# Group norm and attention, one core: query products that go on in a copied PSUM bank, with a new order on VectorE

## What is computed

```python
xn = group_norm(x, gamma, beta)              # 32 groups, eps 0.001
xf = xn.reshape(B, N, C)                     # N = 1024 tokens, C = 512
q = xf @ wq + bq
k = xf @ wk + bk
v = xf @ wv + bv
scores = jnp.einsum('bnc,bmc->bnm', q, k) * C ** (-0.5)
attn = jax.nn.softmax(scores, axis=-1)
out = jnp.einsum('bnm,bmc->bnc', attn, v)
out = out @ wp + bp
return out.reshape(B, H, W, C) + residual    # residual = x
```

## Time and profile before

| | us |
|---|---|
| median of 3 runs (lowest, highest) | 2137.26 (2137.19, 2137.89) |
| the profiled execution's own time | 2139.97 |
| its span in the profile | 2138.3 |

### The profile page before, as it was taken

One profiled execution on the slowest core, in us unless ns is written; L12 is line 12 of the kernel. 1 busy time (PEld: TensorE's weight loads), 2 busy tenths in 40 slices (PEclk: granted clock), 3 DMA queues, 4 the chain that ended last, 5 costly groups with the idle time before them and its releaser, 6 DMA issues.

```text
span 2138.3 us, 28427 instructions
## 1 busy us (share of the span) xinstructions
PE 2099.0 (98%) x9253; PEld 1730.9 (81%) x9253; DVE 1798.7 (84%) x2554; ACT 743.7 (35%) x1216; POOL 877.3 (41%) x475
## 2 busy tenths in 40 slices
PE   7999999999999999999999999999999999999999
PEld 5877888888888888888888788888878888888887
DVE  6898897988979888888888979889788898888865
ACT  4242332423333243332523324233332433335232
POOL 2452442524335244443524425243352434435253
PEclk9999999999999999999999999999999999999999
DMA  8003012030300203012030120303012030120101
GB/s 211 20 11 109 1 54 64 15 103 0 94 24 34 83 0 118 0 49 69 10 108 0 56 62 15 103 0 93 25 34 83 0 118 0 49 69 10 69 1 60
DMA packets 110268, 108.13 MB, mean 51 GB/s; under 512 B 8476, under 2 KB 74016, under 8 KB 110240
## 3 DMA queue, kind: packets, MB, share of 16 engines
q1 hardware_dynamic: 107984, 103.58, 16.0%
q10 hardware_dynamic: 2256, 4.20, 0.8%
HBM read 74.19 MB, written 33.55 MB: 50 GB/s over the span
## 4 chain that ended last, share of the span: by engine, by line
PE 51%; DVE 19%; issue 18%; POOL 7%; ACT 3%; DMA 0%; POOLq 0%; DVEq 0%; ACTq 0%
PE psum L1226 6%; PE psum L1228 6%; PE psum L1227 6%; PE psum L1251 5%; PE psum L1253 5%; PE psum L1252 5%; PE psum L1140 4%; PE psum L1139 4%; PE psum L1137 4%; DVE pt_lo L694 4%; POOL total_part L449 4%; DVE score L869 3%; DVE xn_lo L694 3%; POOL total_part L458 2%; PE psum L1057 2%
## 5 line engine op out<-in xcount | busy, mean ns | idle before, releaser
L1251 PE MATMUL psum<-v_hi,pt_hi 128*128 128x512 f32 x1024 | 401.4, 392 | 20.6 <-DVE pt_lo L694 17.4
L426 POOL TENSOR_TENSOR x_res<-x_res,out_bias 128x512 f32<-128x512 f32 x128 | 201.8, 1600 | 499.1 <-PE psum L1140 371.4
L1252 PE MATMUL psum<-v_lo,pt_hi 128*128 128x512 f32 x1024 | 399.2, 390 | 0.0
L1253 PE MATMUL psum<-v_hi,pt_lo 128*128 128x512 f32 x1024 | 399.0, 390 | 0.0
L694 DVE TENSOR_TENSOR pt_lo<-score,pt_hi 128x512 fp32r<-128x512 f32 x256 | 295.2, 1178 | 28.3 <-POOL total_part L449 25.0
L449 POOL TENSOR_TENSOR total_part<-total_part,score 128x512 f32<-128x512 f32 x192 | 309.1, 1610 | 16.6
L592 ACT ACTIVATE score<-psum 128x512 f32<-128x512 f32 x256 | 152.5, 596 | 342.3 <-PE psum L1228 341.9
L1251 PEld LDWEIGHTS psum<-v_hi,pt_hi 128*128 128x128 f32 x1024 | 192.6, 188 | 68.5 <-DVE pt_lo L694 25.1
L1253 PEld LDWEIGHTS psum<-v_hi,pt_lo 128*128 128x128 f32 x1024 | 192.6, 188 | 40.3
L1252 PEld LDWEIGHTS psum<-v_lo,pt_hi 128*128 128x128 f32 x1024 | 192.7, 188 | 39.1
L1226 PE MATMUL psum<-v_hi,xn_hi 128*128 128x512 f32 x512 | 201.7, 394 | 0.0
(11 more groups left out here) (162 smaller groups left out, 3992.2 us busy)
## 6 DMA issues: line engine op xcount, KB each, us to landing
x_res<-in_x_dram SPq DMA_DIRECT2D x128, 256.0 KB, 3.0
out_dram<-x_res SPq DMA_DIRECT2D x128, 256.0 KB, 2.2
x_blk<-in_x_dram SPq DMA_DIRECT2D x240, 128.0 KB, 3.2
score<-in_x_dram SPq DMA_DIRECT2D x16, 128.0 KB, 8.0
w_q<-in_L_conv_wq_dram SPq DMA_DIRECT2D x1, 1024.0 KB, 5.5
w_k<-in_L_conv_wk_dram SPq DMA_DIRECT2D x1, 1024.0 KB, 7.9
w_v<-in_L_conv_wv_dram ACTq DMA_DIRECT2D x1, 1024.0 KB, 9.1
w_p<-in_L_conv_wp_dram ACTq DMA_DIRECT2D x1, 1024.0 KB, 13.0
```

The source lines that it names most:

```text
L426: last = nc.gpsimd.tensor_tensor(at, at, out_bias[:, first:end], ALU.add)
L1251: nc.tensor.matmul(dst, hi[:, m, queries], v_hi[:, m, :], start=m == 0, stop=False)
L1252: nc.tensor.matmul(dst, hi[:, m, queries], v_lo[:, m, :], start=False, stop=False)
L1253: end = nc.tensor.matmul(dst, lo[:, m, queries], v_hi[:, m, :], start=False, stop=m == NT - 1)
```

## The change

**Queries.** ScalarE copies the first product of each p from its bank into a second bank (`fork`, PSUM to PSUM), and TensorE goes on adding in both: A12 onto the original, S2, S3 and A22 onto the copy. ScalarE keeps two stages of the copy in SBUF (`u2`, `u3`). VectorE adds only S1 to `u3`, and S1 + S4 to `u2`: two chunks of t per p, the other two are read from their banks. So VectorE has 12 instructions for the queries of an image in place of 18, ScalarE has 14 in place of 10. TensorE's 14 products are the same, in another order, with other banks and waits. The banks are `BANK_A = (work[0], work[3])`, `BANK_B = (work[1], work[0])`, `BANK_E = (work[2], work[1])` for p = 0 and 1.

**VectorE's order in image b.** The four `xn_lo_parts` come after all eight `pt_lo_parts` of half 1 and `tile_out` 1 to 3, and no longer between them.

**Image 0.** VectorE adds the bias to the first four residual tiles (`first_residual`) during the scores of half 0, and GpSimd no longer does it. The low parts of the four sums of weights (`block_lo` over `SUMS`) come after `xn_lo_parts` instead of after `v_lo_part` 4; TensorE waits for them in the queries and no longer ahead of its loop.

**Output tile 0.** TensorE waits for the low part of each v tile where it is read, and no longer for v tiles 2 to 6 ahead of the whole tile.

The diff, cut to its core:

```diff
@@ banks and the order of the sums of x
-        BANK_1, BANK_6, BANK_7, BANK_5 = work[2], work[3], work[0], work[1]
+        BANK_A, BANK_B, BANK_E = (work[0], work[3]), (work[1], work[0]), (work[2], work[1])
...
-        SUM_AT = ((1, 1), (0, 1), (0, 0), (1, 0))
+        SUM_AT = ((0, 0), (1, 1), (0, 1), (1, 0))
@@ GpSimd, image
                 top(b, 1)
-                if starts(b):
-                    for i in range(TH):
-                        residual(b, i)
                 totals(b, 1)
@@ ScalarE, queries
+                def fork(p, made):
+
+                    act.wait_ge(s_prod, done + made)
+                    nc.scalar.activation(BANK_B[p], BANK_A[p], ACT.Copy).then_inc(s_fork, 1)
...
+                act.wait_ge(s_free, n * SPLIT + 2)
+                fork(0, 1)
+                keep(u2, 0, 3, s_u2)
+                hi_of_bank(t_hi[0][:, 0, :], BANK_A[0], 0, 4)
+                keep(u3, 0, 5, s_u3)
+
+                act.wait_ge(s_tl, n * 8 + 1)
+                fork(1, 6)
+                hi_of_sum(2, 1)
+                hi_of_bank(t_hi[0][:, 2, :], BANK_B[0], 2, 7)
+                hi_of_sum(0, 2)
+                keep(u2, 1, 9, s_u2)
+                hi_of_bank(t_hi[0][:, 1, :], BANK_A[1], 1, 10)
+                keep(u3, 1, 11, s_u3)
+                hi_of_bank(t_hi[0][:, 3, :], BANK_B[1], 3, 13)
+                hi_of_sum(3, 3)
+                hi_of_sum(1, 4)
@@ VectorE, queries
+                lo_of_bank(BANK_A[0], 0, 1)
+                dve.wait_ge(s_u3, earlier(n) * 2 + 1)
+                sum_with(u3, BANK_E[0], 2, 2)
+                lo_of_sum(2, 2)
+                lo_of_bank(BANK_B[0], 2, 3)
+                dve.wait_ge(s_u2, earlier(n) * 2 + 1)
+                sum_with(u2, BANK_E[0], 0, 8)
+                lo_of_sum(0, 4)
+                lo_of_bank(BANK_A[1], 1, 5)
+                dve.wait_ge(s_u3, earlier(n) * 2 + 2)
+                sum_with(u3, BANK_E[1], 3, 12)
+
+                lo_of_bank(BANK_B[1], 3, 6)
+                lo_of_sum(3, 7)
+                dve.wait_ge(s_u2, earlier(n) * 2 + 2)
+                sum_with(u2, BANK_E[1], 1, 14)
+                lo_of_sum(1, 8)
@@ VectorE, image
+                    if starts(b) and m in (4, 5):
+                        first_residual(m - 4)
                 if more:
                     channel_stats(b + 1)
+                if starts(b):
+                    first_residual(2)
+                    first_residual(3)
...
-                    if starts(b) and m == 4:
-                        for n, at in enumerate(SUMS):
-                            block_lo(at, len(WHOLE) + n + 1, ab_sum[:, at])
...
                 tile_out(b, 0)
+
                 for j in range(KC):
                     pt_lo_parts(b, 1, 2 * j, 2 * j + 2)
-                    if more:
-                        xn_lo_parts(b + 1, j, j + 1)
                     if j:
                         tile_out(b, j)
+                if more:
+                    xn_lo_parts(b + 1, 0, KC)
+                if starts(b):
+                    for n, at in enumerate(SUMS):
+                        block_lo(at, len(WHOLE) + n + 1, ab_sum[:, at])
@@ TensorE, queries (new form whole)
+                past = earlier(n)
+
+                pe.wait_ge(s_free, n * SPLIT + 1)
+                block_product(BANK_A[0], A11, 0, xn_hi, xn_lo, 0, 0)
+
+                pe.wait_ge(s_abl, len(WHOLE) + len(SUMS))
+                pe.wait_ge(s_xsl, past * 4 + 1)
+                block_product(BANK_E[0], S1, 0, xs_hi, xs_lo, 0, 0)
+                pe.wait_ge(s_xsl, past * 4 + 2)
+                pe.wait_ge(s_fork, past * 2 + 1)
+                block_product(BANK_B[0], S2, 0, xs_hi, xs_lo, 1, 1, adds=True)
+                block_product(BANK_A[0], A12, 0, xn_hi, xn_lo, 1, 0, adds=True)
+                pe.wait_ge(s_xsl, past * 4 + 3)
+
+                pe.wait_ge(s_u2, past * 2 + 1)
+                block_product(BANK_B[0], S3, 0, xs_hi, xs_lo, 0, 1, adds=True)
+                block_product(BANK_A[1], A11, 1, xn_hi, xn_lo, 0, 0)
+                pe.wait_ge(s_xsl, past * 4 + 4)
+
+                pe.wait_ge(s_u3, past * 2 + 1)
+                block_product(BANK_B[0], A22, 0, xs_hi, xs_lo, 1, 0, adds=True)
+
+                pe.wait_ge(s_tc, past * 4 + 1)
+                block_product(BANK_E[0], S4, 0, xn_hi, xn_lo, 1, 1, adds=True)
+                pe.wait_ge(s_fork, past * 2 + 2)
+                block_product(BANK_B[1], S2, 1, xs_hi, xs_lo, 1, 1, adds=True)
+                block_product(BANK_A[1], A12, 1, xn_hi, xn_lo, 1, 0, adds=True)
+                pe.wait_ge(s_u2, past * 2 + 2)
+                block_product(BANK_B[1], S3, 1, xs_hi, xs_lo, 0, 1, adds=True)
+
+                pe.wait_ge(s_tl, n * 8 + 3)
+                block_product(BANK_E[1], S1, 1, xs_hi, xs_lo, 0, 0)
+                pe.wait_ge(s_u3, past * 2 + 2)
+                block_product(BANK_B[1], A22, 1, xs_hi, xs_lo, 1, 0, adds=True)
+                pe.wait_ge(s_tc, past * 4 + 3)
+                block_product(BANK_E[1], S4, 1, xn_hi, xn_lo, 1, 1, adds=True)
@@ TensorE, out_tile
-                if i == 0:
-
-                    pe.wait_ge(s_free, n * SPLIT + PLACE[("v", 0, NT - 2)] + 1)
...
-                    if i == 0 and m == NT - 1:
-
-                        pe.wait_ge(s_free, (n + 1) * SPLIT)
+                    if i == 0 and m > 1:
+
+                        pe.wait_ge(s_free, n * SPLIT + PLACE[("v", 0, m)] + 1)
```

More of the change, by code:

```diff
@@ L118, in group_norm_attention @@
         with ExitStack() as sums:
-            sb("above_u1", [P, 2, C], where=sums)
-            u1, u2 = (sb(n, [P, C], where=sums) for n in ("u1", "u2"))
+            sb("above_u2", [P, 3, C], where=sums)
+            u2 = sb("u2", [P, C], where=sums)
             sb("above_u3", [P, NT - 2, C], where=sums)
@@ L123, in group_norm_attention @@
             sb("above_t_sum_1", [P, C], where=sums)
-            t_sum_1 = sb("t_sum_1", [P, KC, BANK], where=sums)
-        t_sum = (t_sum_0, t_sum_1)
+            t_sum = sb("t_sum", [P, KC, BANK], where=sums)
         v_hi = sb("v_hi", [P, NT, C], F32R)
@@ L570, in queries @@
             def queries(n):
[L571 to L582, removed]
-                    act.wait_ge(s_tc, earlier(n) * 6 + 3 * p + 3)
-                    nc.scalar.activation(t_hi[1][:, p, :], t_sum[1][:, p, :], ACT.Copy).then_inc(s_th, 1)
+                done = earlier(n) * PRODUCTS
@@ new lines, in fork, with keep, hi_of_bank @@
+                def fork(p, made):
+                    act.wait_ge(s_prod, done + made)
+                    nc.scalar.activation(BANK_B[p], BANK_A[p], ACT.Copy).then_inc(s_fork, 1)
+                def keep(at, p, made, signal):
+                    act.wait_ge(s_prod, done + made)
+                    nc.scalar.activation(at[:], BANK_B[p], ACT.Copy).then_inc(signal, 1)
+                def hi_of_bank(dst, bank, j, made):
+                    act.wait_ge(s_prod, done + made)
+                    nc.scalar.activation(dst, bank, ACT.Identity, bias=wk_bq[:, j:j + 1]).then_inc(s_th, 1)
@@ new lines, in queries, with lo_of_bank, sum_with @@
+                done = earlier(n) * PRODUCTS
+                def lo_of_bank(bank, j, split):
+                    dve.wait_ge(s_th, n * 8 + split)
+                    nc.vector.scalar_tensor_tensor(out=t_lo[0][:, j, :], in0=bank, scalar=wk_bq[:, j:j + 1],
+                                                   in1=t_hi[0][:, j, :].bitcast(FP32), op0=ALU.add,
+                                                   op1=ALU.subtract).then_inc(s_tl, 1)
+                def sum_with(u, bank, j, made):
+                    dve.wait_ge(s_prod, done + made)
+                    nc.vector.scalar_tensor_tensor(out=t_sum[:, j, :], in0=bank, scalar=wk_bq[:, j:j + 1], in1=u[:],
+                                                   op0=ALU.add, op1=ALU.add).then_inc(s_tc, 1)
@@ L1099, in work_bank @@
                     else:
-                        done = earlier(n)
-                        signal, value = ((s_tl, n * 8 + 5), (s_u2, done * 2 + 2), (s_tc, done * 6 + 5),
-                                         (s_tc, done * 6 + 6))[what[2]]
+                        signal, value = ((s_tc, earlier(n) * 4 + 2), (s_tl, n * 8 + 5), (s_tl, n * 8 + 6),
+                                         (s_tc, earlier(n) * 4 + 4))[what[2]]
                         pe.wait_ge(signal, value)
@@ L1302, in _ @@
                 image(0, True)
-                pe.wait_ge(s_abl, len(WHOLE) + len(SUMS))
             if B > 2:
```

83 lines of the change are left out of this document (15 added, 68 removed).

## The result

| | before | after |
|---|---|---|
| median (lowest, highest), us | 2137.57 (2137.19, 2137.94) | 2191.0 (2190.28, 2192.84) |
| profiled execution's own time | 2139.97 | 2192.84 |
| its span | 2138.3 | 2190.8 |

The changed kernel is slower: ratio 1.0251, 95% interval 1.0234 to 1.0269. The forecast was 2194 for the median and 2197 for the profiled execution.

What follows compares the result with a forecast made beforehand. TensorE, 98% busy, bounds the kernel before; the new A11 wait makes a loop through VectorE and GpSimd set the period. Image 0 -1.2, loop +37, clock +21 give +57 us: 2194 median, 2197 profiled; range 2150 to 2222.

Steps and rivals of the forecast that it cites:

- The place: TensorE at the first query product A11: waits for v_lo 0, 3.9 us per image, about 6 in image 1.
- Rival B: VectorE gets ahead of v tile 1, so A11 never waits; 27 us gained, 2110 us; chance 0.11.
- Rival C: GpSimd's adds miss the totals in every image: loop 130.1 us, no clock loss, 2140 us; chance 0.08.
- The loop: A11, last product, maximum, VectorE and GpSimd, next v_lo 0: 2.67 us above today's period, +37 us over 14 periods.
- the usual lag: VectorE's v_lo 0 is ready about 2.6 us after v tile 1 ends.
- my 0.2 of gain for the order: VectorE's stretch with xn_lo moved behind the pt_lo parts: 0.2 us shorter per image (0 to 0.6).
- The clock: TensorE behind the A11 stall: half clock in seven cases of eight, 1.4 us per image on average, +21 us.
- Rival A: The stalls at A11 do not cool TensorE's clock: +36 us, 2173 us; chance 0.24.
- Image 0 and the start: Moved low parts and adds in image 0 let A11 of image 1 start 1.2 us earlier, after 6 us idle.
- The queries' instructions: VectorE's six fewer gain nothing; ScalarE's PSUM copy, taken as 0.6 us, hides behind a product.
- Rival D: ScalarE's PSUM copy takes well over 1.2 us or a kept copy comes late: 2202 us; chance 0.07.

Runs made afterwards that it cites:

- e10: Kernel before with one constant changed: A11 waits for the low part of v tile 0 though its bank is free; 2189.68 us, ratio 1.0245.
- e5: Kernel after with VectorE's low parts of v tiles 0 and 1 moved ahead of tile_out 6 and 7; 2119.47 us, ratio 0.9917.
- e9: Kernel after with GpSimd's last three residual adds per image cut to 4 of 512 columns; 2121.42 us, ratio 0.9923.
- e3: Kernel after with 12 matmuls that nobody reads ahead of A11's wait in images 1 to 15; 2169.25 us, ratio 1.0149.
- e4: Kernel after with other query banks, A11 on work[2], so v_lo 0 is first needed by the second product; 2188.43 us, ratio 1.0239.
- e6b: Kernel after without GpSimd's last three residual adds per image; 2163.13 us, ratio 1.0119.
- e2: Kernel before with only the change's queries and banks; order, image 0 and output tiles as before; 2192.09 us, ratio 1.0251.
- e8: Kernel of e4b plus a useless 256-column GpSimd add ahead of its row sum in images 1 to 15; 2174.75 us, ratio 1.0163.
- e4b: Same kernel as e4 (kernel after, A11 on work[2]), run again for its trace; 2188.2 us, ratio 1.0237.

## Why the prediction was right, point by point

**The place.** TensorE idle at A11 for `v_lo` 0 in all 15 images; e10 shows that this wait alone costs the 52 us. Rival B, that the signal comes in time, fell. Its condition held nearly in e5 and e9, where the link to `v_lo` 0 is 2.8 to 3.5 us shorter than after's, and there the kernel was faster than before (2119.5 and 2121.4; I had put the rival at 2110). Rival C fell too: the meeting of the earlier trace rows would have made VectorE's link some 2.4 shorter, and in no image of after is it under 87.4.

**The loop.** It was added up as 19.0 + 24.7 + 88.8 + 0.27, the 88.8 being image 6's; with the usual lag it came to 132.6, and 132.48 after my 0.2 of gain for the order. The middle link is 24.66, as in most images before (24.66 to 24.91). The period without the clock is 131.91, 0.57 less. The mis-sized term is the gain of the order: VectorE's turn is shorter by about 0.8 (88.7 on average before, without the one exception of the earlier trace rows, and 87.85 after). In image 7 the eight `pt_lo` are done 12.7 us after GpSimd's first add, for 12.7 forecast, and the row sums start 17.8 after it, for 17.9 and 18.4 before. So the new order gives 0.65 there; my own steps had given 0.55, and I took 0.2 of it without a row that spoke for so little. GpSimd's residual add ends 11.5 after its first one, 1.1 earlier than in the earlier trace rows, again as worked out. Over 14 periods this is 8 us too much in the forecast. The stall at A11 of images 2 to 15 is 3.3 us on average (2.83 to 4.11), for 3.9 forecast: shorter by the same 0.6.

**The clock.** I charged 1.4 us per image, in seven cases of eight; it is 1.75 in 15 of 15, since three of the stretches last 6.83 us. That is 5 us too little, and e3 confirms the size (22 us less than after with 14 of the 15 taken away, and 24.5 with image 0 set apart). Rival A gave 2173 for a clock that stays up, and e3 gave 2169: a right price for a condition that did not hold.

**Image 0 and the start.** -2.8 in place of -1.2; 0.8 of the 2.8 is there already in the part before image 0's scores, where the maximum begins at 100.3 for 101.1. A11's first stall is 5.08, for 6 forecast. How much of this term is the change's own is open: e3 has the same code up to there, and its A11 of image 1 ends the wait at 193.56, 2.6 later than after's.

**The sum.** 57 - 8 + 5 - 1.6 = 52.4, for 52.5 between the spans. Errors of opposite sign make the forecast look better than its terms are: that 2194 stood 3 us from 2191.0 is in part luck. The upper end of the range has a slip without weight: -1 + 37 + 39 + 8 is 83 and not 84.

**The queries' instructions.** No wait within the queries, and the copy from bank to bank takes 0.58 us, for 0.60 assumed (ScalarE, kernel after, image 6):

```profile
863.94 0.58 ACT L571 ACTIVATE psum<-psum 128x512 f32<-128x512 f32 x1 [5.62 <-PE psum L1170]
```

Rival D fell. It has a small remainder that I had not seen: the copy writes the bank of v tile 1, and in e5, where A11 hardly waits, it costs up to 0.4 in most images by waiting for `v_lo` 1.

**What was missed** in the expectations of the runs, not in the prediction: in e4 and e6b I changed one link of the loop and held the others fixed. Both times the others moved, through GpSimd's reductions over partitions: what they hold up on VectorE (e4), and what comes late behind them on GpSimd (e6b).

## What to carry to other kernels

When the engine that sets the time waits for another one's signal only thanks to a few instructions of slack (here three products, 4.1 us), look how late that signal is in each iteration before using up the slack: if the late engine's turn depends on the first engine's results, the wait closes a loop, and everything saved elsewhere on the first engine turns into idle time there. Before moving a bank or a buffer, list which of its users' releases is the last to come, and give the first instruction of the next stage one that has long been free. The whole gain of a good edit (here the order, 19 us) can be hidden by a bad one beside it, so time the parts one by one.

## What the runs showed of the hardware that I had not expected

**The clock after short stalls.** Stalls of nearly the same length left the clock at full or halved it. In e2 7 of 15 at A11 halved it, among them one of 2.57 us, and one of 2.85 did not; in e10 5 of 15 did; of after's (2.83 to 5.08 us) all 15. A stall of 1.8 us in image 1 halved it in e9 and not in e2. In the kernel before, one of 3.0 us for `dev` did not the earlier trace rows. The stalls ahead of S1 in e8 halved it in 12 of 15 images, one of 1.88 us among them, and in e4b in 11 of 15, where four of 2.27 to 2.66 did not. So no one length decides by itself in these runs. A stretch of 3.41 us cost about 1.6 and one of 6.83 about 2.9. The Trainium skill (TensorE: Matmul & The Clock Gate, "HAM oscillation — how this bites in real kernels") warns of a wait that recurs in every iteration and cools the array every time; the kernel after agrees in 15 images of 15, e2 and e10 only in 7 and in 5.

**GpSimd's start-up.** Its first tensor instruction after a reduction over partitions comes about 7 us later (7.10 in e9, 6.69 in image 7 of after, 7.56 in the earlier trace rows; 6.6 to 7.9 at 45 of the 47 such places of the kernel after), and a reduction 5.7 to 6.2 after a tensor instruction (45 of 47). Where no other tensor instruction has come between, this time is paid behind the signal (7.3 in e6b). What fills it, no run shows.

**The shared path.** A reduction over partitions holds a maximum of VectorE that lasts 0.69 us alone for 2.91 or 4.76 us, until about a microsecond before the reduction's end. Which of the two it is, was decided by a shift of some 0.3 to 0.5 us (e4b, e8). The Trainium skill (SBUF — State Buffer, "Who interferes with whom") calls the shared port an exclusive lock; the waiting of the maxima and e9 (a total at 0.29 beside the tiny adds) agree with that.

**ScalarE into PSUM.** A copy of 128x512 out of PSUM takes 0.58 us into PSUM, against 0.60 into SBUF.
